# Where a token block's weights are made: before it, under an image attention, or at its own start

## The reference, cut to what matters

```python
x = conv_block(x)                   # 4 images, 256 channels, 32 x 32: group norm, 1x1 q, k, v,
                                    # softmax(q.k / 16) over 1024 positions, 1x1 projection, + x
t = to_tokens(x)                    # (4, 1024, 256)
t = t + attn_ref(ln(t), q_w, k_w, v_w, o_w, gate_w, up_w, down_w, norm1_w, norm2_w)
                                    # rms norm, q and k through log / exp maps of a ball,
                                    # 8 heads, causal; then silu(h gate^T) * (h up^T) down^T
t = t + ffn_ref(ln(t), gate_w, w1, b1, w2, b2)
                                    # 8 experts, each token goes to 2: w1[e] (1024 x 256), w2[e] (256 x 1024)
```

## Time and profile before

| | us |
|---|---|
| median of 3 runs | 1532.42 |
| lowest, highest | 1531.77, 1536.89 |
| the profiled execution | 1548.29 |
| its span (first to last instruction) | 1546.5 |

### The profile page before, as it was taken

One profiled execution on the slowest core, in us unless ns is written; L12 is line 12 of the kernel. 1 busy time (PEld: TensorE's weight loads), 2 busy tenths in 40 slices (PEclk: granted clock), 3 DMA queues, 4 the chain that ended last, 5 costly groups with the idle time before them and its releaser, 6 DMA issues. The chain is left out here.

```text
span 1546.5 us, 27783 instructions
## 1 busy us (share of the span) xinstructions
PE 1217.2 (79%) x9365; PEld 820.5 (53%) x9366; DVE 767.9 (50%) x1460; ACT 702.5 (45%) x1330; POOL 485.7 (31%) x411
## 2 busy tenths in 40 slices
PE   3989999452988698869777985440699999999992
PEld 1546666331334333433343343340588888888882
DVE  3755555156464657556655454542244444444441
ACT  3565454155567666756675652320232332333321
POOL 2021000101960294049305910557032332332331
PEclk9999999776999899979998996555899999999996
DMA  4576989824630662085108305994433433433326
GB/s 136 136 205 183 251 246 234 239 86 77 169 110 8 112 181 82 14 147 168 55 14 168 119 35 149 246 258 136 67 47 53 54 44 51 54 45 51 54 34 224
DMA packets 350675, 183.50 MB, mean 119 GB/s; under 512 B 271104, under 2 KB 337920, under 8 KB 350464
## 3 DMA queue, kind: packets, MB, share of 16 engines
q1 hardware_dynamic: 317056, 124.66, 35.3%
q0 software_dynamic: 25184, 56.64, 15.0%
q10 hardware_dynamic: 8352, 1.08, 0.5%
HBM read 38.66 MB, written 83.11 MB: 79 GB/s over the span
## 5 line engine op out<-in xcount | busy, mean ns | idle before, releaser
L2074 ACT ACTIVATE moe_hid<-moe_hbank,moe_b1T 128x256 f32<-128x256 f32 x312 | 130.2, 471 | 265.5 <-PE moe_hbank L2031 265.5
L2031 PE MATMUL moe_hbank<-moe_xT,l_w1T 128*128 128x256 f16 x1872 | 212.7, 274 | 45.7 <-DMA moe_xT<-rows_scratch 44.4
L2031 PEld LDWEIGHTS moe_hbank<-moe_xT,l_w1T 128*128 x1872 | 183.9, 98 | 68.2 <-issue 46.1
L2010 POOL DMA_INDIRECT acc_scratch<-moe_y,moe_meta x78 | 122.5, 1570 | 310.9 <-DVE moe_y L2101 288.2
L2046 PE MATMUL moe_ybank<-l_w2T,moe_hid_hi 128*128 x1248 | 206.4, 273 | 0.3 <-DVE moe_hid_lo L2088 0.3
L1111 ACT ACTIVATE block_probs<-block_bank 128x1024 f32<-128x1024 f32 (+1 forms) x192 | 144.8, 808 | 81.2 <-PE block_bank L870 67.2
L2046 PE MATMUL moe_ybank<-l_w2T,moe_hid_lo 128*128 x624 | 170.1, 273 | 0.0
L2086 DVE TENSOR_SCALAR moe_hid_hi<-moe_hid 128x2048 f16<-128x2048 f32 x39 | 47.8, 1227 | 203.4 <-ACT moe_hid L2074 203.4
L2046 PEld LDWEIGHTS moe_ybank<-l_w2T,moe_hid_hi 128*128 128x128 f16 x1248 | 122.1, 98 | 14.7 <-issue 0.6
L867 PE MATMUL block_bank<-block_qkT 128*128 128x512 f16 (+3 forms) x384 | 95.6, 338 | 39.6 <-DMA block_qkT<-block_stack 28.3
L732 POOL COPY block_stack<-block_stack 128x512 f16<-128x512 f16 x16 | 11.2, 700 | 315.1 <-ACT block_stack L1095 315.1
(11 more groups left out here) (354 smaller groups left out, 2550.2 us busy)
## 6 DMA issues: line engine op xcount, KB each, us to landing
rows_scratch<-l_blank SPq DMA_DIRECT2D x32, 1056.0 KB, 5.3
block_raw<-in_L_ffn_w POOLq DMA_DIRECT2D x32, 512.0 KB, 4.6
w_parts<-block_raw_hi POOLq DMA_DIRECT2D x32, 256.0 KB, 4.4
w_parts<-block_raw_lo POOLq DMA_DIRECT2D x32, 256.0 KB, 4.8
l_xs<-in_x SPq DMA_DIRECT2D x8, 512.0 KB, 7.2
x_scratch<-conv_mixed SPq DMA_DIRECT2D x8, 512.0 KB
block_t<-x_scratch SPq DMA_DIRECT2D x16, 256.0 KB, 4.1
acc_scratch<-block_res SPq DMA_DIRECT2D x16, 256.0 KB, 2.2
```

Source lines behind the costliest of these rows:

```text
L2010: pool.indirect_dma_start(acc, bass.IndirectOffsetOnAxis(ap=meta[r][:, t, 0:1].bitcast(U32), axis=0), y[r % 2][:, t, :], None, compute_op= ...
L2031: last = pe.matmul(hbank[:, c, :], w1T[:, e, wp, k, c * P:(c + 1) * P], xT[q][:, xp * CC + k, :], start=n == 0, stop=n == 5)
L2074: act.activation(hid[q][:, c, :], hbank[:, c, :], ACT.Gelu, bias=b1T[:, e, c:c + 1], scale=1.0 / (GAIN * GAIN)).then_inc(S["gelu_done"], 1)
```

## The change

The seven token weights are loaded, split and turned in `conv_attention`. They are cut in ten chunks of 128 x 512. SP loads chunk c in step 14 + c, ACT makes its high part and DVE its low part at the end of step 16 + c, and SP turns it by DMA transposes (four of 128 x 256, or two of 128 x 512 for the last two chunks) in steps 17 to 24, 27 and 28. Their place in SBUF is that of the image, which is no longer needed where they land. PE no longer turns weights, and `first_front` has no strips.

24 of the 32 expert pieces are split by GpSimd in `conv_attention` (5, 2, 4 and 13 after the bias of images 0 to 3), 8 in the token block (3, 3, 2 and 0).

10 of the 34 fills stay in the image attention (in steps 1, 3, ... 19), 24 go to the token block, eight behind the transposes of each of the images 0 to 2. SP's loop over images is written out there.

Waits for constants and norm weights in the token block stand where they are used.

```diff
+    def run(self, pool, first, last, end):          # class WeightPieces; body as L739 to L752 before
+        for n in range(first, last):
...
@@ conv_attention, SP
+                def load_chunk(c):
+                    u, o, k = chunks[c]
+                    if c >= 2:
+                        sp.wait_ge(nat_lo_done, c - 1)
+                    sp.dma_start(nat[c % 2][:, :].rearrange("p (o i) -> p o i", o=k),
+                                 whole[u].rearrange("(o p) i -> p o i", p=P)[:, o:o + k, :]).then_inc(nat_loaded[c % 2], 16)
+                def turn_chunk(c):
+                    u, o, k = chunks[c]
+                    sp.wait_ge(nat_lo_done, c + 1)
+                    for i in range(k):
+                        for part, nat_part in zip(token_parts[u], (nat_hi, nat_lo)):
+                            sp.dma_start_transpose(part[:, :, (o + i) * P:(o + i + 1) * P],
+                                                   nat_part[c % 2][:, i * 512 // k:(i + 1) * 512 // k]).then_inc(nat_turned[c % 2], 16)
...
-                    for dst, src in fills[n::STEPS]:
+                    for dst, src in fills[n // 2:n // 2 + 1] if n % 2 else ():
                         sp.dma_start(dst, src).then_inc(filled, 16)
+                    if 0 <= n - LOAD_AT < len(chunks):
+                        load_chunk(n - LOAD_AT)
+                    if n in TURN_AT:
+                        turn_chunk(TURN_AT.index(n))
@@ conv_attention, ACT, DVE and GpSimd
+                def weight_high(c):
+                    act.wait_ge(nat_loaded[c % 2], 16 * (c // 2 + 1))
+                    if c >= 2:
+                        act.wait_ge(nat_turned[c % 2], 64 * (c // 2))
+                    act.activation(nat_hi[c % 2][:, :], nat[c % 2][:, :], ACT.Copy, scale=W_GAIN).then_inc(nat_hi_done, 1)
...
+                    if 0 <= n - SPLIT_AT < len(chunks):
+                        weight_high(n - SPLIT_AT)
...
+                ends = (0, 5, 7, 11, EARLY)
+                pieces.load(pool, 0)
+                pieces.load(pool, 1)
                 for b in range(B):
...
+                    pieces.run(pool, ends[b], ends[b + 1], EARLY)
+                pieces.stored(pool, EARLY)
...
+                def weight_low(c):
+                    dve.wait_ge(nat_hi_done, c + 1)
+                    dve.scalar_tensor_tensor(nat_lo[c % 2][:, :], nat[c % 2][:, :], W_GAIN, nat_hi[c % 2][:, :],
+                                             ALU.mult, ALU.subtract).then_inc(nat_lo_done, 1)
@@ token_block
-                each = len(splits) // B
+                late_ends = (EARLY, EARLY + 3, EARLY + 6, *(len(pieces.splits) for _ in range(2)))
...
+                def fill(b):
+                    for dst, src in fills[len(fills) * b // (B - 1):len(fills) * (b + 1) // (B - 1)]:
+                        sp.dma_start(dst, src).then_inc(filled, 16)
...
                 for pr in range(PAIRS):
                     turn(0, pr)
-                with sp.Fori(1, B) as b:
+                fill(0)
+                for b in range(1, B):
...
+                    if b < B - 1:
+                        fill(b)
...
                 def first_front():
-                    for n in range(QKV_STRIPS):
-                        weight_strip(n)
                     for pr in range(PAIRS):
                         h_turned(0, pr)
-                        if pr == 0:
-                            pe.wait_ge(S["w_lo"], QKV_STRIPS)
                         qkv(0, 2 * pr)
                         qkv(0, 2 * pr + 1)
-                        for n in strips_with(pr):
-                            weight_strip(n)
```

More of the change, by code:

```diff
@@ L301, in conv_attention @@
         mixed = [s.sb(f"mixed{i}", [P, HALF, C]) for i in range(2)]
+        nat = [s.sb(f"nat{i}", [P, 512]) for i in range(2)]
+        nat_hi, nat_lo = ([s.sb(f"nat_{n}{i}", [P, 512], F16) for i in range(2)] for n in ("hi", "lo"))
         qk_bias = s.sb("qk_bias", [P, 2, CC])
@@ L357, in _ @@
                 sp.wait_ge(filled, 16 * len(fills))
+                for q in range(2):
+                    sp.wait_ge(nat_turned[q], TURNED_PER_SLOT)
             @block.tensor
@@ L584, in _ @@
                         low_part(b + 1, u)
+                    if 0 <= n - SPLIT_AT < len(chunks):
+                        weight_low(n - SPLIT_AT)
                 for n in range(STEPS - LAG, STEPS):
@@ L604, with token_block @@
 BARRIER = 4096.0
-def token_block(nc, x1, t2, ident, ident_h, weights, norm1_w, norm2_w, splits):
+def token_block(nc, x1, t2, ident, ident_h, w, t1, norm1_w, norm2_w, fills, filled, pieces):
     SCALE = 2.0 / (float(HD) ** 0.5 * QK_GAIN ** 2)
@@ L683, in token_block @@
         S = {n: s.sem(n) for n in names}
-        raw_loaded, parts_stored = ([s.sem(f"{n}{i}") for i in range(2)] for n in ("raw_loaded", "parts_stored"))
-        raw_scaled, raw_hi_done, raw_lo_done = (s.sem(n) for n in ("raw_scaled", "raw_hi_done", "raw_lo_done"))
         FRONT_DVE, FRONT_ACT, LATE_DVE = 19, 6, 4
-        def split_of(n):
-            unit, k = strips[n]
-            if unit < 3:
-                return *(part[:, k, unit * D:(unit + 1) * D] for part in w["qkv"]), D
-            return *(part[:, k, :] for part in w[("gate", "up", "down", "o")[unit - 3]]), weights[unit].shape[0]
         def o_bank(pr):
@@ L1030, in _ @@
                 first_front()
-                pe.wait_ge(S["consts"], CONSTS)
                 attention(0, 1)
@@ L2206, in build @@
         ident, ident_h = s.sb("ident", [P, P]), s.sb("ident_h", [P, P], F16)
+        filled = s.sem("filled")
+        front = ExitStack()
+        outer, s = s, Scope(nc, front, "front")
+        pieces = WeightPieces(s, outer, splits)
+        blank = s.sb("blank", [P, GT, ROW], F16)
+        make_blank_rows(nc, blank)
+        blocks_v = rows.rearrange("(n t p) r -> t p n r", p=P, t=GT)
+        fills = [(blocks_v[t][:, n:min(n + 8, BLOCKS), :],
+                  blank[:, t:t + 1, :].bitcast(U32).to_broadcast((P, min(8, BLOCKS - n), ROW // 2))) for n in range(0, BLOCKS, 8) for t in range(GT)]
+        EARLY_FILLS = 10
+        shared = s.sb("shared", [P, B * CC * T * 2], F16)
+        names = ("q", "k", "v", "o", "gate", "up", "down")
+        token_weights = [(n, p[f"L1_attn_{n}_w"]) for n in names]
+        at, parts = 0, {}
+        for n, k, f in (("qkv", CC, 3 * D), ("o", CC, D), ("gate", CC, FF), ("up", CC, FF), ("down", FC, D)):
+            parts[n] = [shared[:, at + i * k * f:at + (i + 1) * k * f].rearrange("p (k f) -> p k f", k=k) for i in range(2)]
+            at += 2 * k * f
+        token_parts = {**{n: [part[:, :, i * D:(i + 1) * D] for part in parts["qkv"]] for i, n in enumerate("qkv")},
+                       **{n: parts[n] for n in names[3:]}}
+        t1 = shared[:, (B - 1) * CC * T * 2:B * CC * T * 2].bitcast(F32).rearrange("p (t d) -> p t d", t=NT)
         with ExitStack() as ctx:
@@ L2232, in build @@
             first_group_norm(nc, norms[0])
-            conv_attention(nc, xs, x1, scale, shift, norms[1], fills, w, bias, bias_loaded, fold_bias, ident)
+            conv_attention(nc, xs, x1, scale, shift, norms[1], fills[:EARLY_FILLS], w, bias, bias_loaded, fold_bias, ident,
+                           token_weights, token_parts, pieces)
             s.clear()
-        token_block(nc, x1, acc[0:B * T, :], ident, ident_h, [p[f"L1_attn_{n}_w"] for n in ("q", "k", "v", "gate", "up", "down", "o")],
-                    p["L1_attn_norm1_w"], p["L1_attn_norm2_w"], splits)
+        token_block(nc, x1, acc[0:B * T, :], ident, ident_h, parts, t1, p["L1_attn_norm1_w"], p["L1_attn_norm2_w"], fills[EARLY_FILLS:], filled, pieces)
+        front.close()
         with ExitStack() as ctx:
```

149 lines of the change are left out of this document (52 added, 97 removed).

## The result

| | us |
|---|---|
| before, median of 4 runs | 1534.17 |
| changed kernel, median of 4 runs | 1558.36 (1557.23 to 1561.71) |
| ratio | 1.0161, interval 1.0135 to 1.0186 |
| its profiled execution, span | 1558.40, 1556.6 |

The change makes the kernel slower by 24 us. The forecast of 1526 (1508 to 1541) was wrong in sign and in range.

What follows compares the result with a forecast made beforehand. PE was taken to bound steps 7 to 23, the DVE and ACT chain from step 24. Image attention +6.6, seam +0.4, token block start -10, later images -3.4 gave -6.4: 1541.9 profiled, 1526.0 median, range 1508 to 1541.

Steps and rivals of the forecast that it cites:

- The turning loop, +4: Image attention: reusing a chunk's buffer takes a round of 7.7 to 8.7 us against the step; +4 us, bounds 0 to 30.
- Rival three: SP's turning loop sets the pace if small transposes land in 6.5 us, not 3.4; +30 in the loop, 1544.0 total; 14%.
- The attention's end behind 312: Sign that the forecast is wrong: image attention ending after 312 us would point to the turning loop.
- Low parts of chunks, +6.8: Steps 16 to 23: DVE's chunk low part 0.65 plus stalls 1.0, less 0.8 of room, times eight; +6.8 us.
- Steps 24 and 25, +3.3: Image attention, steps without room on DVE: low part 0.65 plus stalls 1.0, twice; +3.3 us.
- Early steps, 0: Early image attention: fewer fills give -2, stalls of DVE by five POOL pieces +2; 0 us, bounds -6 to +5.
- The rule on the shared port: DVE and GpSimd share ports as an exclusive lock; whoever comes second waits for the other's whole instruction.
- rival two: POOL's instructions block DVE for their whole length: 12 us in steps 16 to 23, total 1528.8; 14%.
- the tail: End of image attention: no fill or chunk in steps 29 to 31, so the last low part's transpose issues at once; -8 us.
- the seam: Between the last residual and the token block: clearing 47 semaphores in place of 41; +0.4 us.
- the start of the token block: Earlier norm weights and no weight strips: first copy of q and k -7.9, pairs' loop -2.1; -10 us.
- the images: Later images of the token block: pieces end early, so L1478's excess of 1.4 and 1.9 goes; -3.4 us.

Runs made afterwards that it cites:

- Compute only: Changed kernel with all 32 pieces in the token block, plus a stand-in for 24 early pieces: full elementwise work, transfers of 8 columns; ratio 1.0028.
- spread, no pieces: Changed kernel with joint high/low transposes, no early pieces, chunks split in two of three steps, turning ahead of the load; 1513.90 us, ratio 0.9858.
- transfers only: Changed kernel with all 32 pieces in the token block, plus 24 early pieces' full transfers, one-column memsets replacing elementwise work; ratio 1.0209.
- the paced stand-in: Full transfers of 24 early pieces without their elementwise work, with 180 one-column memsets a piece in place of 30; ratio 1.0195.

## Why the prediction was wrong, point by point

**The step that failed is "The turning loop, +4".** It took "three waits for issues of 64 KB transposes at 0.7 (an estimate below the 1.28 of a 256 KB one)", and added a landing. Two things were wrong. The 64 KB transpose takes 1.25, as much as the 256 KB one; the bound from above was the right value, and I had chosen the one in favour of the change. And the round was written as a chain of latencies, when the queue also issues two transposes of the probabilities, every second step a fill, in the same time: 8.1 us of issues a step without pieces (8.4 with their gaps), 8.7 to 13.3 and once 20.6 with them, for steps of 6.7 to 8. From step 18 to step 26 the row maxima lose 36.9 us (7.7 behind before at step 18, 44.6 at step 26), nine times the term. The granted clock is no rival to this: it falls to 0.77 in 222 to 262, but PE is busy in only 26.5 of these 40 us, while SP's queue stands nearly back to back. Rival three named the place and the side, with +30, but gave it 14%. Its mechanism, longer landings in a loop, is a small part of what happened. Landings did rise to 4.6 while the pieces ran, past the 4.3 from which it was to decide. But the loop kept SP waiting for 3.8 us in all, and the runs that loosened it (the turning first, four buffers) gave at most 10 us of the 37 back. The attention's end behind 312, which the prediction had named as its sign of the loop, therefore came for another reason than the one named.

**"Low parts of chunks, +6.8" and "Steps 24 and 25, +3.3".** Without stalls the first would have been 0, since 0.65 is below the room of 0.8; all of the 6.8 came of the stalls. Where PE is the bound they cost nothing: with the weights left back the whole pieces add -0.2 us from step 15 to step 31. Compute only adds 2.0 there, but in that run SP's queue sets the pace and could hide more. Single stalls are there (the low part of the probabilities is 1.58 us on the mean of 32 for a median of 1.23) but they decide nothing. With chunks that never wait (spread, no pieces) it is 219.7 us from step 0 to step 31, for 218.5 with the fills alone moved: the 0.6 in front of each of the row maxima 27 and 28 (6.1 for 5.5), and nothing from the eight chunks in steps up to 23. So the 0.65 of a low part was right, and the stall added to it was not.

**"Early steps, 0".** The stalls are there instead. This term was -2 for fewer fills and +2 for five pieces. From step 0 to step 15 the moved fills gave -3.5 (fills only) and the pieces cost 10.6, so the row maxima are 7.1 us behind before. Compute only accounts for 6.4 of the 10.6 and transfers only for 4.0. The step that grows most is 12 (13.89 for 10.06), where DVE makes the low parts of a normalised image from two SBUF operands while POOL works, with nothing behind which to hide: these two instructions take 5.08 us for 2.35, and the low part of the probabilities ahead of them 2.67 for 1.23.

**The rule on the shared port** (the Trainium skill, "SBUF — State Buffer", "Who interferes with whom"), as rival two had it, put 12 us in steps 16 to 23. The trace shows waits of the kind that it describes, up to 2.68 us for an instruction of 1.23, but where PE is the bound they cost nothing (the -0.2 above). They cost in the early steps, to which the rival gave nothing of its own.

**Right were** the tail (-8 forecast, -8.8 measured), the seam (+0.4, +0.4), the start of the token block (-10 forecast; -10.2 from the block's first load to image 0's last duplicate), and the sign and near size of the images (-3.4, -2.1; L1478 itself went from 17.7 to 13.4 us in all). POOL's last early piece began at 252.22, where 255 was the forecast for the end of all pieces, so nothing spilled over. The -10 was right in part by luck: it was -7.9 up to the first copy and -2.1 behind it, and -9.1 and -1.1 were measured. The -2.1 rested on a misread row: the 0.76 of the low parts in the earlier trace rows is for the two of them together (x2), so the term should have been -1.4.

By its own measured terms the sum is 44.6 - 8.8 + 0.4 - 10.2 - 2.1 = 23.9, for 24.2 between the medians.

**Open.** That POOL's transfers, and not its elementwise work, make an issue on SP take 2 to 6 us is shown by the runs that have one without the other (1.31 and 2.98 at the median). Through what they do it is not shown; how much is bytes and how much the number of transfers in flight was not told apart, and the paced stand-in failed to size it.

## What to carry to other kernels

Before work is moved under a stage, add up the issues of each queue in one period of it, all instructions of that queue, old and new, and compare the sum with the period. A queue that never shows as busy on an engine's line can bound the stage all the same. Then ask whether the issues keep their length under the traffic that the same change adds: here 18.7 of 46.8 us came only of the two together. And where a price must be taken from another size, take the measured one for anything that sits in a queue the critical path needs.

## What the runs showed of the hardware

A DMA transpose of 16-bit data took 1.25 us to issue at 64 KB (x36), 1.29 at 128 KB (x18) and 1.24 to 1.31 at 256 KB. With POOL's transfers beside it (1.05 MB a piece, a piece each 8.1 to 8.7 us) the issue of a 256 KB transpose took 2.98 at its median and up to 6.2, and one plain load 5.07; with POOL's elementwise work alone beside it the median stayed at 1.31. Landings of the 64 KB transposes were 4.6 with and 2.4 without that traffic. The routing stage, whose code was the same in all kernels, took 131.7 to 133.1 us in most profiled executions and 139.8 to 148.9 in five.
